# Attention inside a fused attention and expert kernel: 40 score units a head merged to 34 of 512 columns, causal mask added by VectorE in PSUM, attention's order written anew

## The reference

```
q, k, v = (proj(Wq, bq), proj(Wk, bk), proj(Wv, bv))
scores = einsum('bhqd,bhkd->bhqk', q, k) / sqrt(HD) + slopes * distances
scores = where(causal, scores, finfo.min)
attn = softmax(scores, axis=-1)
ctx = einsum('bhqk,bhkd->bhqd', attn, v)
x + (ctx @ Wo + bo) + experts(xn)
```

## Time and profile before

| | us |
|---|---|
| median of 3 runs | 2099.18 (2096.61 to 2100.73) |
| the profiled execution | 2096.1 |
| its span, first to last instruction | 2094.3 |
| granted TensorE clock, mean | 0.97 |
| one step of attention (30 steps in 1083.23 us) | 36.11 |

### The profile page before, as it was taken

How to read it: one execution, slowest core, us unless ns; L and a number is a source line. 1 busy time by engine, 2 the same in 40 slices (tenths; PEclk the granted TensorE clock), 3 DMA queues, 4 the chain that set the end, 5 groups by cost and what they waited for, 6 DMA issues and landing times. The chain is left out here.

```text
span 2094.3 us, 40489 instructions
## 1 busy us (share of the span) xinstructions
PE 1988.7 (95%) x9182; PEld 1441.7 (69%) x9183; DVE 1366.0 (65%) x3106; ACT 1346.4 (64%) x2891; POOL 1363.9 (65%) x1262
## 2 busy tenths in 40 slices
PE   6999996799999999999999999999989989999996
PEld 4888885477777777777777777777746666666664
DVE  5454443888878888887878787888838843333332
ACT  4323321299999999999999999999972223333332
POOL 3110112188888888888989888888977625555554
PEclk9999998599999999999999999999999999999998
DMA  7577666423323232332324242323117755555554
GB/s 228 201 247 247 228 215 207 104 53 83 90 74 99 74 99 72 83 90 69 104 52 119 54 119 52 97 55 78 30 43 239 230 175 95 96 99 97 94 99 70
DMA packets 118487, 243.95 MB, mean 116 GB/s; under 512 B 15920, under 2 KB 52656, under 8 KB 112144
## 3 DMA queue, kind: packets, MB, share of 16 engines
q1 hardware_dynamic: 100464, 206.09, 33.8%
q0 software_dynamic: 17984, 37.38, 10.0%
HBM read 139.28 MB, written 104.21 MB: 116 GB/s over the span
## 5 line engine op out<-in xcount | busy, mean ns | idle before, releaser
L905 POOL TENSOR_TENSOR probs_lo<-probs,probs_hi 128x512 fp32r<-128x512 f32 (+2 forms) x864 | 1018.4, 1205 | 182.0 <-ACT probs L937 175.3
L936 ACT ACTIVATE probs_hi<-s_ps 128x512 fp32r<-128x512 f32 (+2 forms) x1024 | 642.5, 627 | 116.5 <-PE s_ps L1158 106.9
L937 ACT ACTIVATE probs<-s_ps 128x512 f32<-128x512 f32 (+3 forms) x1120 | 628.5, 586 | 4.7 <-PE s_ps L1155 1.1
L972 DVE TENSOR_REDUCE m_part<-m_ps 128x1 f32<-128x512 f32 x768 | 500.2, 685 | 59.3 <-PE m_ps L1137 58.0
L1155 PE MATMUL s_ps<-q_st,k_st 100*128 100x512 f32 (+1 forms) x880 | 330.2, 391 | 11.7 <-DVE probs_lo L981 5.2
L1137 PE MATMUL m_ps<-k_st,q_st 98*128 98x512 f32 (+2 forms) x880 | 325.3, 408 | 12.0 <-DVE m_part L969 6.6
L1170 PE MATMUL o_ps<-probs_hi,v_split 128*96 128x512 f32 x704 | 286.8, 407 | 0.1
L969 DVE CUSTOM_DVE_ANT_0 m_ps<-m_ps,mask_row 128x128 f32<-128x128 f32 (+3 forms) x512 | 250.8, 499 | 52.0 <-PE m_ps L1137 41.5
L1172 PE MATMUL o_ps<-probs_lo,v_split 128*96 128x512 f32 x704 | 265.9, 378 | 0.0
L1530 POOL DMA_INDIRECT out<-y,tile_rows x71 | 114.3, 1610 | 170.1 <-issue 97.9
L1155 PEld LDWEIGHTS s_ps<-q_st,k_st 100*128 100x128 f32 x880 | 168.1, 191 | 74.3 <-issue 18.0
(11 more groups left out here) (192 smaller groups left out, 3655.4 us busy)
## 6 DMA issues: line engine op xcount, KB each, us to landing
v_d<-v_rows SPq DMA_DIRECT2D x7, 3072.0 KB, 10.0
v_split<-v_d SPq DMA_DIRECT2D x22, 768.0 KB
k_st<-k_hi_d SPq DMA_DIRECT2D x44, 256.0 KB
q_st<-q_hi_d SPq DMA_DIRECT2D x44, 256.0 KB
xs<-in_x SPq DMA_DIRECT2D x8, 1024.0 KB, 6.8
xn_d<-xs SPq DMA_DIRECT2D x8, 1024.0 KB, 12.1
q_hi_d<-qk_hi SPq DMA_DIRECT2D x32, 256.0 KB, 7.2
q_lo_d<-qk_lo SPq DMA_DIRECT2D x32, 256.0 KB, 7.6
```

Of the source, the lines that this page charges most:

```text
L905: nc.gpsimd.tensor_tensor(*low_operands(u), ALU.subtract).then_inc(lo_ready_pool, 1)
L936: nc.scalar.activation(probs_hi[:, u % P_RING, 0:w], scores, ACT.Exp, scale=SCALE)
L937: nc.scalar.activation(scores if KIND[u] == "Q" else probs[:, u % P_RING, 0:w], scores, ACT.Exp, scale=SCALE).then_inc(p_ready, 1)
L972: V.tensor_reduce(top, scores, AX.X, ALU.max).then_inc(m_taken, 1)
```

## The change

- `score_units` replaces the list: 34 units a head, all of 512 columns. The narrow diagonal parts are paired in one bank: 128 with 384 columns of the same query block, and 256 with 256 of two neighbouring blocks. The parts are still 40 matmuls a head, with the same keys and queries; the value products follow the parts.
- The mask matmul is gone, with its two bf16 operands. `mask_scores` on DVE adds the mask in place in `s_ps`, one instruction for a unit with one or two diagonal blocks; ACT waits for that (`s_masked`) instead of the matmul (`s_ready`). DVE does it at the letter S.
- `KIND` goes from 27 P, 5 Q, 8 W to 25 P, 4 Q, 5 W. `BACK['V']` goes from 6 to 8, `P_RING` from 8 to 9, with a fixed list of places (`P_SLOT`) and a start value of 17 for `pv_done`.
- `ORDER` and `KIND` are written anew.
- Some small tensors of the token counting move to other places, so that the ninth buffer fits.

```diff
-S_UNITS = [(qc, kt) for qc in range(S // CH) for kt in range(TPC * (qc + 1))]
+def score_units():
+    def whole(qc, kt):
+        return [(qc, kt, CH * qc, CH, 0)]
+    def from_diagonal(qc, i, at):
+        return (qc, TPC * qc + i, CH * qc + P * i, CH - P * i, at)
+    units = []
+    for a in range(0, S // CH, 2):
+        b = a + 1
+        units += [whole(a, kt) for kt in range(TPC * a + 1)] + [[from_diagonal(a, 3, 0), from_diagonal(a, 1, P)], whole(b, 0)]
+        units += [[from_diagonal(a, 2, 0), from_diagonal(b, 2, CH // 2)]]
+        units += [whole(b, kt) for kt in range(1, TPC * b + 1)] + [[from_diagonal(b, 3, 0), from_diagonal(b, 1, P)]]
...
-KIND = "PPPWPPPWPPWWPPPQPPPPPQPWPWPWPPQPPQPQPPPW"
+KIND = "PPWPPPPPPWPPPPQPPPWPPQPQPPWPPWQPPP"
...
-BACK = {'L': 4, 'V': 6, 'O': 1}
+BACK = {'V': 8, 'L': 4, 'O': 1}
 HEADS_RING = 3
-P_RING = 8
+P_RING = 9
+P_SLOT = [*range(8), *range(9), *range(8), *range(9)]
...
             def weights(n, u):
-                act.wait_ge(s_ready, NS * n + u + 1)
-                act.wait_ge(pv_done, NS * n + u + 1)
+                if s_diagonals(u):
+                    act.wait_ge(s_masked, masked_count(n, u))
+                else:
+                    act.wait_ge(s_ready, NS * n + u + 1)
+                act.wait_ge(pv_done, PV_START + NS * n + u - units_between(u) + 1)
...
+            def mask_scores(n, u):
+                at = s_diagonals(u)
+                if not at:
+                    return
+                dve.wait_ge(s_ready, NS * n + u + 1)
+                if len(at) == 1:
+                    blocks = s_ps[:, S_BANK[u], at[0]:at[0] + P].unsqueeze(1)
+                else:
+                    blocks = s_ps[:, S_BANK[u], 0:2 * (at[1] - at[0])].rearrange("p (a c) -> p a c", a=2)[:, :, 0:P]
+                V.tensor_tensor(blocks, blocks, t["consts"][:, 2:3, :].to_broadcast([P, len(at), P]), ALU.add
+                                ).then_inc(s_masked, 1)
...
-                last = nc.tensor.matmul(s_ps[:, S_BANK[u], CH - w:CH], k_st[r][0:ROWS, kt * P:(kt + 1) * P],
-                                        q_st[r][0:ROWS, q0:q0 + w], start=True, stop=not diagonal)
-                if diagonal:
-                    last = nc.tensor.matmul(s_ps[:, S_BANK[u], CH - w:CH - w + P], ident_r, mask_s, start=False, stop=True)
+                for qc, kt, q0, w, at in S_UNITS[u]:
+                    last = nc.tensor.matmul(s_ps[:, S_BANK[u], at:at + w], k_st[r][0:ROWS, kt * P:(kt + 1) * P],
+                                            q_st[r][0:ROWS, q0:q0 + w], start=True, stop=True)
                 last.then_inc(s_ready, 1)
```

More of the change, by code:

```diff
@@ L57 @@
 ROW_BIAS, ROW_MAX, ROWS = 96, 98, 100
-S_UNITS = [(qc, kt) for qc in range(S // CH) for kt in range(TPC * (qc + 1))]
+def score_units():
[9 more added lines that the diff above has]
+        units += [whole(b, kt) for kt in range(1, TPC * b + 1)] + [[from_diagonal(b, 3, 0), from_diagonal(b, 1, P)]]
+    assert TPC == 4
+    return units
+S_UNITS = score_units()
 NS = len(S_UNITS)
@@ L67, with s_diagonals, masked_count @@
 M_SLOTS = NM + 1
[L70 to L74, removed]
+def s_diagonals(u):
+    return [at for qc, kt, q0, w, at in S_UNITS[u] if q0 == kt * P]
+def masked_count(h, u):
+    diagonal = [bool(s_diagonals(v)) for v in range(NS)]
+    return sum(diagonal) * h + sum(diagonal[:u + 1])
 def m_span(m):
@@ L89, in m_diagonal @@
     return k0 + w == (qt + 1) * P
-LAST_UNIT = [max(u for u in range(NS) if S_UNITS[u][0] == qc) for qc in range(S // CH)]
-KIND = "PPPWPPPWPPWWPPPQPPPPPQPWPWPWPPQPPQPQPPPW"
-ORDER = ("SMMVMMLMVMVLSVMSVMMSSMSMVSMVMMLOLSSVMVMSVMSVMOSVLMSMSVLSVLMSMMLVSDVVSMVVSMSLMMLSVLMVSVMLSDLLLLVLSVLM"
-         "MOSSVLMSVLMSSMVMSVSMLMVMDVSMVSVMSVXLSVDSWLVLVSVDSLOVVSLVSL")
-BACK = {'L': 4, 'V': 6, 'O': 1}
+LAST_UNIT = [max(u for u in range(NS) for part in S_UNITS[u] if part[0] == qc) for qc in range(S // CH)]
+KIND = "PPWPPPPPPWPPPPQPPPWPPQPQPPWPPWQPPP"
+ORDER = ("SMMMVVVMVMMVLSSMVMLLSMVMMVOVSLMSMVSLSMLMLVSMSMVSLMLMLVMMOVSMSSVMMSVMVMDOSLMVLLSVSMVSVMSMVSMMVSMVMSLD"
+         "LVSLMLLVMDLSMVSMMSSVMSVLSVXWVSLVLLDSOVSVLLS")
+BACK = {'V': 8, 'L': 4, 'O': 1}
 HEADS_RING = 3
-P_RING = 8
+P_RING = 9
+P_SLOT = [*range(8), *range(9), *range(8), *range(9)]
+assert len(P_SLOT) == NS
 M_BUFS, S_BUFS = 3, 3
@@ L137, in bank_before, with units_between @@
     return (at, 0) if at is not None else (max(v for v in range(NS) if S_BANK[v] == S_BANK[u]), 1)
+def units_between(u):
+    return next(d for d in range(1, NS + 1) if P_SLOT[(u - d) % NS] == P_SLOT[u])
+PV_START = max(units_between(u) for u in range(NS))
 VS = 3 * HD
@@ L701, in attend @@
 def attend(nc, sb, ps, sem, t):
-    ident, ident_r, mask_s, pairs = t["ident"], t["ident_r"], t["mask_s"], t["pairs"]
+    ident, pairs = t["ident"], t["pairs"]
     with ExitStack() as ctx:
@@ L748, in attend @@
         s_ready = sem(ctx, "s_ready")
+        s_masked = sem(ctx, "s_masked")
         p_ready = sem(ctx, "p_ready")
@@ L1086, in step_n @@
                         continue
+                    if kind == "S":
+                        mask_scores(n, u)
                     if kind == "O":
@@ L1159, in score_tile @@
                 last.then_inc(s_ready, 1)
             def value_products(n, r, u):
[L1162 to L1177 removed]
+                if KIND[u] == "W":
+                    pe.wait_ge(p_ready, NS * n + u + 1)
+                else:
+                    pe.wait_ge(lo_ready_dve if KIND[u] == "Q" else lo_ready_pool, low_count(n, u))
@@ new lines, in value_products @@
+                for qc, kt, q0, w, at in S_UNITS[u]:
+                    if kt == 0:
+                        pe.wait_ge(o_added, QCS * n + qc + 1)
+                    dst, values = o_ps[0:VS, qc % 2, q0 - qc * CH:CH], v_split[r][:, kt, :]
+                    here = (slice(None), P_SLOT[u], slice(at, at + w))
+                    if KIND[u] == "W":
+                        last = nc.tensor.matmul(dst, values.bitcast(F32), probs[here],
+                                                start=(kt == 0), stop=True, skip_group_check=True)
+                    else:
+                        nc.tensor.matmul(dst, values, probs_hi[here], start=(kt == 0), stop=True, skip_group_check=True)
+                        last = nc.tensor.matmul(dst, values, probs_lo[here], start=False, stop=True, skip_group_check=True)
@@ L1178, in value_products @@
                 last.then_inc(pv_done, 1)
-            pe.sem_inc(pv_done, P_RING)
+            pe.sem_inc(pv_done, PV_START)
             pe.wait_ge(hot_ready, 1)
```

63 lines of the change are left out of this document (19 added, 44 removed).

## The result

| | before | after |
|---|---|---|
| median of 12 runs, us | 2098.4 (2095.7 to 2102.1) | 2106.2 (2103.2 to 2108.6) |
| ratio, with its 95% interval | | 1.0036 (1.0027 to 1.0045) |
| profiled execution; its span | 2096.1; 2094.3 | 2107.7; 2105.9 |
| one step of attention | 36.11 | 36.34 |

The forecast was 2072, with a range up to 2097: the time is 34 us over the one and 9 over the other, and the sign is wrong. The page of the kernel after, against the earlier trace rows: TensorE has 512 instructions less and 16 us less of busy time in a longer span, DVE 71 us more.

The account below looks back on a forecast made before the run. TensorE was taken as the bound, with 2% of holes. A step was 34.25 us of TensorE work + 0.40 holes + 0.60 wait at S33 = 35.25, 0.86 less, 27 us over 31 steps: 2072 us, range 2054 to 2097.

Parts of the forecast that it names:

- The ninth buffer costs nothing and removes waits: POOL's products: its work is never within a microsecond of its product, so the extra buffer is free.
- Between S4 and S31 ACT has no slack, so each microsecond that it idles there is one of the step: Middle of a head: late masks there lengthen the step one for one; it decides from 0.86 us a step on.
- The signs of being wrong that I had named: Attention: ACT waiting for DVE between S4 and S31 over a microsecond a head, or PE holes at the maxima.
- the case without waits: Rival at the head's end: ACT early enough at S33, 34.65 us a step, 2054 us in all; chance 0.12.
- the 0.40 taken for small holes: PE's step: small waits and the loop's turn, 0.40 us, kept as before.
- S33: Last score of a head, using S31's bank: PE waits 0.60 us there for ACT in each head.
- The bounds that I gave for a pair: Merged units on PE: a 128-column part ahead of 384 costs 0.05 us extra, bounds 0 and 0.08 each.
- The mask matmuls and their followers: PE: 16 masks at 0.04 us plus slowed followers, 1.6 us a step saved; bounds 0.64 and 1.7.
- The ping-pong of the third O with S32: Head's end: ACT copies, DVE adds then masks, ACT idles about 1.1 us, which should fall into a hole.
- The stall of 0.40 us at the maxima: Start of a head: three maxima take 1.05 us instead of 0.65 as DVE holds their banks; should go.
- ACT takes over halfway: Rival: mask waits idle ACT; if 0.8 us a step remain, the time is as before, 2097 us; chance 0.10.
- Slower: Rival: five mid-head masks each 0.5 us late on DVE, 37.1 us a step, 2130 us; chance 0.12.

Follow-up runs that it names:

- a_store_first: Changed kernel with SP issuing the first O's store ahead of the eight loads: step 35.58 us against 36.34, ratio 0.9932 to the kernel before.
- a_product_moved: a_store_first with one float32 value product moved ahead of the head's last score, V lagging seven: step 34.97 us, ratio 0.9840 to the kernel before.
- a_parts: a_store_first with the wide part of a merged unit first, in scores and products: step 35.58 us, ratio 0.9869 to the kernel before.
- b_no_mask: Kernel before without its 16 mask matmuls a head, weights unmasked and exponent scaled down: step 35.56 us against 36.11, ratio 0.9897.
- a_no_mask: Changed kernel without masks on DVE, ACT waiting for the matmul alone: step 36.22 us against 36.34, ratio 0.9992 to the kernel before.

## Why the prediction was wrong

**The step that failed** is in the part on POOL and on the order: "The ninth buffer costs nothing and removes waits", and the search for tight places, which went through PE's banks and ACT's exponentials only. The change moved the last V of a head and the second O, and with them SP's loads and the store that ACT's copy waits for; neither the queue of SP nor the two buffers of the sums stood in the count, although the loads' wait for the last V was in my own description of the kernel. Price: 0.6 to 0.76 us a step (a_store_first), some 20 us. The rule that would have priced it was in the text, "Between S4 and S31 ACT has no slack, so each microsecond that it idles there is one of the step": ACT idled 1.02 us there in the head shown, 0.94 a head in the mean, and the step lost 0.6 to 0.76. The signs of being wrong that I had named, ACT waiting for DVE between S4 and S31 and holes at the maxima, did not appear: ACT's two waits for masks stand at S32 and S1, and what failed was an idle ACT for another reason.

**The rest of the miss** is 0.33 us a step (35.58 against 35.25), and in a_product_moved again 0.32 (34.97 against the 34.65 of the case without waits). In a_product_moved PE is idle for 0.2 of 1040 us, so what is missing there is no wait: it is in the distances between TensorE's starts, that is in the terms of the sum or in the 0.40 taken for small holes. The merged units are not it. Their two parts take 0.30 us where nothing was waited for (910.57 to 910.87 in a_product_moved), as forecast with 0.234 + 0.05. Only where PE has waited do they take more: in after S33 takes 914.49 to 914.89 = 0.40 us and S18 936.82 to 937.21 = 0.39. The bounds that I gave for a pair, 0 and 0.08, were too narrow there. It isn't the order of the parts either (a_parts). Which term was too small stays open.

**Right by its own steps:**
- The mask matmuls and their followers, 1.6 us on TensorE; b_no_mask shows 512-column followers at 0.234. It also shows that 1.6 us less on one engine is worth 0.55 where nothing else is changed.
- S33: 0.60 forecast, 0.61 measured (a_product_moved), of which 0.50 was idle time; that the last hundredths agree is luck. The signature came too, PE held before the last score of a head for ACT, 0.38 us by the row.
- The ping-pong of the third O with S32: 1.16 us at 916.08, forecast about 1.1, and free (a_no_mask). Likewise ACT's second long wait, 1.18 at S1.
- The stall of 0.40 us at the maxima is gone; DVE's wait for maxima has fallen from 31.3 to 3.0 us.
- POOL's subtractions of 512 are still 1295 ns, and the masks on DVE 292 ns for 128 columns and 441 for 256, as taken from the earlier trace rows:

```profile
L933 POOL TENSOR_TENSOR probs_lo<-probs,probs_hi 128x512 fp32r<-128x512 f32 x414 | 522.6, 1295 | 78.8 <-ACT probs L967 78.7
...
L1023 DVE TENSOR_TENSOR s_ps<-s_ps,consts 128x256 f32<-128x256 f32 x98 | 43.2, 441 | 0.6
...
L1023 DVE TENSOR_TENSOR s_ps<-s_ps,consts 128x128 f32<-128x128 f32 x65 | 19.0, 292 | 0.5
```

**Wrong in size:** the first head was 4.6 us shorter, not half a microsecond longer. A part of it can be counted: with V eight behind, its step lacks eight products of a head before instead of six, two W among them, 4.6 us of TensorE instead of 2.2 by the forecast's costs. That is 2.4 of the 4.6, and the 1.06 that the sum has for every step come on top; the rest is not explained, and no run tests it. Some of it comes back behind the last step, where the lagging products stand. In the last head I took nothing; it is 2.5 us longer, with masks behind DVE's split of Wo (a_no_mask: 4 us less than after):

```profile
1551.08 3.24 DVE L1167 TENSOR_TENSOR wo_lo<-wo_raw,wo_hi 128x2048 fp32r<-128x2048 f32 x1
...
1556.11 0.60 ACT L966 ACTIVATE probs_hi<-s_ps 128x512 fp32r<-128x512 f32 x1 [1.36 <-DVE s_ps L1023]
```

The output stage's 2.8 us were not followed up.

**The rivals.** "ACT takes over halfway" had the right effect, 0.8 us a step given back through an idle ACT between S4 and S31, at a time of 2097, and the wrong cause: not the masks. "Slower" had the mechanism of ACT's missing slack and again the masks as its cause; they came in time. I had put my doubts on the engine whose work grew (DVE) and none on the queue whose work stayed the same and was only moved. And a range that ends at the case "0.8 us remain" left no room for that case together with 3.7 us of another start, 2.5 of the last head and 2.8 of the output.

## What to carry to other kernels

When an order of work is written anew, list for every engine, and for the queue engine too, what each wait is released by, and where that now stands: here a small store issued behind a group of loads landed 7.7 us after its issue and 11 us after its data was ready (924.16), and a ring of two buffers then stopped an engine that has no slack. Count such a release in time from its issue to the next use of its buffer, 10.8 us here before and 6.7 after, as one counts banks of PSUM. Work taken from the bound engine is worth only what the next engine leaves: 1.6 us gave 0.55 in the old order, while in the new order, with its two waits removed, the step fell by 1.14 us.

## What the runs showed that was not expected

- Of the two stores of a sum (64 KB the larger), issued behind 2.3 MB of loads on the same queue engine, the last one landed 7.7 us after its issue (927.50 to ACT's start at 935.21). With the stores first, no one waits for them.
- The same changed kernel had its start of attention at 373.0 and at 369.6, and an output stage of 127 and, on another chip, of 175 us, while the step of attention was the same within 0.14 us. For a change inside one stage, a distance within that stage tells more than the total time.
- Two parts of 128 and 384 columns take 0.39 to 0.40 us where TensorE has stood before them, 0.16 more than one matmul of the same 512 columns, and 0.30 where it has not.
